# Cross attention L2 written anew: 32-row feature and norm products, new order on all engines

## What is computed

```python
q = _split_heads(queries @ Wq.T); k = _split_heads(keys @ Wk.T); v = _split_heads(values @ Wv.T)
q2 = jnp.sum(q * q, axis=-1); k2 = jnp.sum(k * k, axis=-1)
qk = jnp.einsum('bhsd,bhtd->bhst', q, k)
g_dist = jnp.sqrt(jnp.maximum(q2[..., :, None] + k2[..., None, :] - 2.0 * qk, 0.0)) / DIST_SCALE
compat = (1.0 + g_dist) ** (-(D_INTRINSIC + ALPHA))
N_R = jnp.sum(compat, axis=-1); N_C = jnp.sum(compat, axis=-2)
K_tilde = (N_R ** (-A_EXP))[..., :, None] * compat * (N_C ** (-A_EXP))[..., None, :]
value_weights = K_tilde / jnp.maximum(jnp.sum(K_tilde, axis=-1, keepdims=True), EPS)
attn = jnp.einsum('bhst,bhtd->bhsd', value_weights, v)
...
x = x + _L2_xattn_ref(_layernorm(x, axis=-1), ctx_1024, ctx_1024, ...)
```

## Time and profile before

| | us |
|---|---|
| median of 3 runs | 4875.21 (4873.07 to 4876.48) |
| the profiled execution | 4871.57 |
| its span, first to last instruction | 4869.7 |
| PE busy | 4274.2 (88%) |
| DVE busy | 3812.1 (78%) |
| ACT busy | 3566.7 (73%) |
| POOL busy | 3203.4 (66%) |

### The profile page before, as it was taken

The page is one execution under the profiler, slowest core; times in us unless marked ns, Lnnn a source line. Parts: engine busy times, 40 slices in busy tenths (PEclk is TensorE's granted clock), DMA queues, the critical chain, the costliest instruction groups (busy, mean ns, idle before and its releaser), DMA issues. The chain is left out here.

```text
span 4869.7 us, 153128 instructions
## 1 busy us (share of the span) xinstructions
PE 4274.2 (88%) x50692; PEld 2794.5 (57%) x50694; DVE 3812.1 (78%) x9246; ACT 3566.7 (73%) x13078; POOL 3203.4 (66%) x4063
## 2 busy tenths in 40 slices
PE   6949899988999889998899979998899986677775
PEld 3426566664666646665566646666466664444433
DVE  4779899965999569993899839996599955777488
ACT  6938788974889658884788838887488865777335
POOL 2512399974999569993899929997399952322162
PEclk8969999998999999999899989999999998888986
DMA  2000000000000000000000000000000000000000
GB/s 58 0 19 0 5 2 0 0 19 6 2 0 0 19 7 1 0 0 21 5 0 0 1 24 2 0 0 19 6 2 0 0 19 1 0 0 0 1 27 18
DMA packets 36457, 34.77 MB, mean 7 GB/s; under 512 B 11591, under 2 KB 31301, under 8 KB 35141
## 3 DMA queue, kind: packets, MB, share of 16 engines
q1 hardware_dynamic: 36164, 31.14, 2.2%
HBM read 29.03 MB, written 2.10 MB: 6 GB/s over the span
## 5 line engine op out<-in xcount | busy, mean ns | idle before, releaser
L2479 ACT ACTIVATE local_prob<-ps,local_shift_by 128x128 f32<-128x128 f32 x3072 | 1081.2, 379 | 10.0 <-DVE local_shift_by L2559 9.9
L2407 POOL TENSOR_TENSOR local_qk<-local_qk,local_rsin 128x512 f32<-128x512 f32 x768 | 969.8, 1274 | 57.7 <-DVE local_rsin L2584 57.7
L2414 POOL TENSOR_TENSOR local_qk<-local_qk,local_inv 128x512 f32<-128x512 f32 x768 | 794.4, 1046 | 125.9 <-ACT local_inv L2498 125.3
L2718 PE MATMUL ps<-local_wqkv,local_xsT 128*128 128x512 f32 x1536 | 831.2, 627 | 50.5 <-DVE local_rsin L2584 24.9
L2421 POOL TENSOR_TENSOR local_prob<-local_prob,local_rs 128x512 f32<-128x512 f32 x768 | 792.4, 1044 | 12.6 <-DVE local_rs L2566 12.6
L2479 ACT ACTIVATION_READ_ACCUMULATOR local_prob<-ps,local_shift_by 128x1 f32 x3072 | 673.3, 219 | 0.0
L2573 DVE TENSOR_TENSOR local_qk<-ps,local_cos_t 128x512 f32<-128x512 f32 x768 | 525.3, 684 | 95.3 <-ACT local_sq L2487 92.9
L2559 DVE TENSOR_REDUCE local_shift_by<-ps 128x4 f32<-128x512 f32 x768 | 524.6, 683 | 83.6 <-PE ps L2794 83.6
L2584 DVE TENSOR_TENSOR local_rsin<-ps,local_sin_t 128x256 f32<-128x256 f32 x1536 | 572.1, 414 | 0.0
L2487 ACT ACTIVATE local_sq<-ps 128x512 f32<-128x512 f32 x768 | 467.2, 608 | 101.2 <-PE ps L2718 78.3
L2591 DVE TENSOR_REDUCE local_ss<-local_sq 128x8 f32<-128x512 f32 x768 | 513.1, 669 | 4.9 <-ACT local_sq L2487 4.9
(11 more groups left out here) (332 smaller groups left out, 8849.1 us busy)
## 6 DMA issues: line engine op xcount, KB each, us to landing
local_wqkv<-L_ffn_Wqkv SPq DMA_DIRECT2D x7, 1536.0 KB, 6.7
local_wo<-L_ffn_Wo SPq DMA_DIRECT2D x7, 512.0 KB, 7.3
out<-quantised_res SPq DMA_DIRECT2D x8, 256.0 KB, 2.3
local_w<-L_ffn_W SPq DMA_DIRECT2D x6, 341.0 KB
L_cross_decay<-c_decay SPq DMA_DIRECT2D x1, 1024.0 KB, 12.0
local_w<-L_ffn_W SPq DMA_DIRECT2D x12, 64.0 KB
load_raw<-L_ffn_w SPq DMA_DIRECT2D x8, 64.0 KB, 2.1
local_b<-L_ffn_b SPq DMA_DIRECT2D x24, 0.5 KB
```

Source lines behind the costliest of these rows:

```text
L2407: nc.gpsimd.tensor_tensor(qk[w][:, j, :, :], qk[w][:, j, :, :], rsin[j % 2][:, :, :], ALU.add).then_inc(rot_ready, 1)
L2414: nc.gpsimd.tensor_tensor(qk[w][:, j, :, :], qk[w][:, j, :, :], bcast(inv[:, w, 8 * j:8 * j + 8].unsqueeze(2), [P, 8, LH]), ALU.mult).then ...
L2479: last = nc.scalar.activation(prob[w][:, g, j, :], ps[:, 4 + g % 2, j * P:(j + 1) * P], ACT.Exp, bias=shift_by[:, w, h:h + 1], accum_out=s ...
L2718: nc.tensor.matmul(proj_bank(j), xsT[w][:, :], wqkv[:, 512 * j:512 * j + 512], start=True, stop=True).then_inc(proj_ready, 1)
```

## The change

`cross_attention` is removed and `cross_attention_L2` is written in its place; L0, L1, L3 and all other phases stay as they are, but for their line numbers. In the new phase:

- Features and norms are apart. `fixed` holds k and -2q in full height, `aux` holds the norms and ones, eight rows a head of which two are used. PE's `scores` makes, for a pair of head groups, two 32-row products of features and then two 32-row products of norms into the same banks. POOL makes `spread` and `spread_aux`, 128 by 512 each, with the mask `head_rows`, and also the squares (`squared`).
- The evacuations out of PSUM are shared anew: `xnT`, k, -2q, v and the norms are all taken by DVE, the norms in one operation of 256 columns; ACT reads PSUM only for the logarithm of the row sums. The blocks `vbd` and `nbd` are written by POOL.
- The row sums have a place of their own (`ROWS`, in bank 5 beside `OUT`) and are made two steps ahead of the values. The end of the normalisation is a reciprocal of the weighted sum, `limit`, which takes the smaller of it and 1e12 times the row root, and one product with the values; `num`, `den` and its clamp are gone.
- `work` has two sets, the stages of a tile are spread over more steps, and each engine's order in a step is new. The constant `tile_rows` is gone, `aux_one` replaces two constants, and the selection matrices are new.

```diff
+            def squares(b, w, live):
+                if live(b):
+                    pool.wait_ge(fixed_ready, b + 1)
+                    pool.wait_ge(src_ready, b + 1)
+                    wait(pool, norms_ready, b - 1)
+                    nc.gpsimd.tensor_tensor(squared[:, w, :, :], fixed[:, w, :, :], fixed[:, w, :, :], ALU.mult).then_inc(squares_ready, 1)
...
+            def block_values(b, w, live):
+                if live(b):
+                    pool.wait_ge(rsum_ready, b + 1)
+                    pool.wait_ge(vraw_ready, b + 1)
+                    wait(pool, pv_ready, b - 1)
...
+            def step(n, u, live):
+                v = 1 - u
+                spread_heads(n - 1, v, live)
+                spread_norms(n - 1, v, live)
+                block_values(n - 3, v, live)
+                fetch_context(n, u, live)
+                squares(n, u, live)
+                add_output_bias(n - 4, u, live)
+            sequence_loop(pool, NB, 0, 4, step)
...
+            def step(n, u, live):
+                v = 1 - u
+                columns(n - 4, u, live)
+                second_log(n - 3, v, 0, live)
+                root(n - 3, v, 1, live)
+                powers(n - 3, v, 0, live)
+                log_variance(n, u, live)
+                second_log(n - 3, v, 1, live)
+                first_log(n - 2, u, 0, live)
+                powers(n - 3, v, 1, live)
+                log_rows(n - 4, u, live)
+                log_variance2(n - 6, u, live)
+                over_deviation(n, u, live)
+                root(n - 2, u, 0, live)
+                rows(n - 4, u, live)
+                first_log(n - 2, u, 1, live)
+                log_columns(n - 3, v, live)
+                over_deviation2(n - 6, u, live)
+            sequence_loop(act, NB, 0, 6, step)
...
+            def evacuate_norms(b, w, live):
+                if live(b):
+                    dve.wait_ge(norms_ready, b + 1)
+                    wait(dve, scores_ready, 4 * (b - 1))
+                    nc.vector.tensor_tensor(aux[:, w, :, :], NORMS.rearrange("p (t q) -> p t q", t=2),
+                                            bcast(env["aux_one"][:, :].unsqueeze(2), [P, 2, P]), ALU.add).then_inc(aux_ready, 1)
...
+            def limit(b, w, live):
+                if live(b):
+                    dve.wait_ge(nrow_ready, b + 1)
+                    dve.wait_ge(recip_ready, b + 1)
+                    wait(dve, oT_ready, b - 1)
+                    nc.vector.scalar_tensor_tensor(cut[:, w, :], nrow[:, w, :], 1e12, recip[:, w, :],
+                                                   ALU.mult, ALU.min).then_inc(cut_ready, 1)
...
+            def residual(b, w, live):
+                if live(b):
+                    dve.wait_ge(out_ready, b + 1)
+                    dve.wait_ge(xb_ready, b + 1)
+                    nc.vector.tensor_tensor(tile_of(X, b), xb[:, w, :], OUT, ALU.add).then_inc(x_ready, 1)
...
+            def step(n, u, live):
+                v = 1 - u
+                statistics(n + 6, u, live)
+                evacuate_values(n + 4, u, live)
+                aggregate(n + 6, u, live)
+                evacuate_x(n + 5, v, live)
+                floor(n + 4, u, 0, live)
+                floor(n + 4, u, 1, live)
+                floor(n + 4, u, 2, live)
+                evacuate_spread(n + 5, v, live)
+                evacuate_fixed(n + 5, v, live)
+                column_sums(n + 3, v, 0, live)
+                floor(n + 4, u, 3, live)
+                evacuate_norms(n + 5, v, live)
+                column_sums(n + 3, v, 1, live)
+                norm(n + 6, u, live)
+                one_over_rows(n + 2, u, live)
+                residual(n + 1, v, live)
+                limit(n + 2, u, live)
+                statistics2(n + 1, v, live)
+                evacuate_heads(n + 2, u, live)
+                aggregate2(n + 1, v, live)
+                end_norm(n, u, live)
+            sequence_loop(dve, NB, 6, 0, step)
...
+            def scores(b, w, half, live):
+                if live(b):
+                    pe.wait_ge(spread_ready, b + 1)
+                    pe.wait_ge(spread_aux_ready, b + 1)
+                    pair = (2 * half, 2 * half + 1)
+                    for g in pair:
+                        wait(pe, work_ready, 4 * (b - 1) + g + 1)
+                    for g in pair:
+                        r = slice(32 * g, 32 * g + 32)
+                        nc.tensor.matmul(scores_of(g), fixed[r, w, 0, :], spread[w][r, :, :], start=True, stop=False)
+                    for g in pair:
+                        r = slice(32 * g, 32 * g + 32)
+                        nc.tensor.matmul(scores_of(g), aux[r, w, 0, :], spread_aux[w][r, :, :], start=False,
+                                         stop=True).then_inc(scores_ready, 1)
+
+            def row_sums(b, w, live):
+                if live(b):
+                    pe.wait_ge(prob_ready, 2 * b + 2)
+                    wait(pe, lnrow_ready, b)
+                    wait(pe, x_ready, b - 1)
...
+            def output(b, w, live):
+                if live(b):
+                    pe.wait_ge(oT_ready, b + 1)
+                    wait(pe, x_ready, b)
+                    wait(pe, lnrow_ready, upto(b + 2, NB))
+                    nc.tensor.matmul(OUT, oT[:, w, :], wo[:, :], start=True, stop=True).then_inc(out_ready, 1)
+
+            def step(n, u, live):
+                v = 1 - u
+                weighted_values(n + 1, v, live)
+                norms(n + 4, u, live)
+                output(n, u, live)
+                turn_x(n + 5, v, live)
+                row_sums(n + 2, u, live)
+                scores(n + 4, u, 0, live)
+                scores(n + 4, u, 1, live)
+                project(n + 5, v, live)
+            sequence_loop(pe, NB, 5, 0, step)
```

More of the change, by code:

```diff
@@ L3120, in residual_layers @@
                "X": sb("X", [P, NB * P]), "XN": sb("XN", [P, NB * P]), "Y": sb("Y", [P, NB * P])}
-        for name, shape in (("ident", [P, P]), ("shift", [P, P]), ("head_rows", [P, HG]), ("tile_rows", [P, 2, 8]),
-                            ("aux_sel_fixed", [P, P]), ("aux_sel_spread", [P, P]), ("aux_one_fixed", [P, 1]),
-                            ("aux_one_spread", [P, 1]), ("ones_bd", [P, HG, 32]), ("rotary1", [P, 4, LH]),
+        for name, shape in (("ident", [P, P]), ("shift", [P, P]), ("head_rows", [P, HG]),
+                            ("aux_sel_fixed", [P, P]), ("aux_sel_spread", [P, P]), ("aux_one", [P, 2]),
+                            ("ones_bd", [P, HG, 32]), ("rotary1", [P, 4, LH]),
                             ("band_f", [P, P]), ("band2_f", [P, LH + 96])):
@@ L3178, in residual_layers @@
                   lambda: cross_attention_L1(nc, env, a), layers1,
-                  lambda: cross_attention(nc, env, a, "L2"), lambda: gated_ffn(nc, env, a, 0, "L2"),
+                  lambda: cross_attention_L2(nc, env, a), lambda: gated_ffn(nc, env, a, 0, "L2"),
                   lambda: cross_attention_L3(nc, env, a)]
@@ L3202, in shape_constants @@
     c["c_head_rows"] = ((i[:, None] // DH) % HG == np.arange(HG)[None, :]).astype(f)
-    feature = (i[:, None] // DH) % 8 == np.arange(8)[None, :]
-    norm = i[:, None] % 32 == np.arange(8)[None, :]
-    low_rows = (i < 64)[:, None]
-    c["c_tile_rows"] = np.stack([np.where(low_rows, feature, norm), np.where(low_rows, norm, feature)], 1).astype(f)
-    head_of_row = np.where(i % 32 < 8, i % 32 + 8 * (1 - i // 64), -1)
-    mine = head_of_row[None, :] == (i // DH)[:, None]
-    low = (i % 64 < 32)[None, :]
-    c["c_aux_sel_fixed"] = (mine & low).astype(f)
-    c["c_aux_sel_spread"] = (mine & ~low).astype(f)
-    c["c_aux_one_fixed"] = ((i % 64 >= 32) & (i % 32 < 8)).astype(f)[:, None]
-    c["c_aux_one_spread"] = ((i % 64 < 32) & (i % 32 < 8)).astype(f)[:, None]
+    mine = (i // DH)[:, None] == (i // DH)[None, :]
+    c["c_aux_sel_fixed"] = (mine & (i % DH == 0)[None, :]).astype(f)
+    c["c_aux_sel_spread"] = (0.25 * (mine & (i % DH == 1)[None, :])).astype(f)
+    c["c_aux_one"] = np.stack([i % DH == 1, i % DH == 0], 1).astype(f)
     ones = np.zeros((P, HG, 32), f)
```

932 lines of the change are left out of this document (290 added, 642 removed).

## The result

The changed kernel takes 4785.87 us (median of 4 runs, 4781.67 to 4787.8), the kernel before 4874.18 (4873.07 to 4876.48) beside it: a ratio of 0.9815, 95% interval 0.9803 to 0.9826. The forecast was 4786.0 in a range of 4712 to 4845. The profiled execution took 4787.02 us with a span of 4785.2.

What follows compares the result with a forecast made beforehand. The prediction took a PE and DVE loop through `residual` and `row_sums` as the bound: terms summing to 11.4 us plus 0.57 for the clock, 12.0 a tile; 63 + 28 x T gave 399 us, median 4786, range 4712 to 4845.

Steps and rivals of the forecast that it cites:

- What bounds the kernel now: Old phase: a loop of waits through POOL's spread, the context copy behind it and PE's projections, about 14.4 us a tile.
- The new loop: PE and DVE take turns once a tile: `row_sums` waits for `residual`, which stands behind `evacuate_norms`; 11.4 us.
- Its terms: Pieces of the PE and DVE loop: 1.89 + 0.61 + 0.07 + 2.95 + 0.95 + 4.02 + 0.94 = 11.4 us a tile.
- The slack of 0.25 us on the parallel branch: From the end of `project`, DVE needs 2.25 us to reach `evacuate_norms`, PE 2.5 to give the norms; 0.25 left.
- The clock: PE's 2.8 us gap before `row_sums`: one tile in three pays 1.7 us at half clock, 0.57 on average.
- Start and end: Pipeline two steps deeper: start-up 43 us, tail 20, so phase = 63 + 28 x T.
- The rule that I set against the row: Skill's 3.07 times speedup for four row tiles: scores 2.2 us and T 9.6, where the row gave 4.02.
- Changing the tiling mode: Skill's rule that mode changes drain TensorE: three more changes, some 0.2 us each, 0.6 us a tile, 17 in all.
- VectorE beside POOL: Skill's rule that a 2-port VectorE operation waits for a whole GpSimd instruction: `norm` could wait for `spread_norms`, sum same within tenths.
- Engines: Work a tile in the new phase: DVE some 9.0 us, ACT 9.1 to 9.9, POOL under 6.
- ACT's waits for `work`: Sign to look for in the new phase: ACT waits for `work` 1 us or less a tile.
- Engines' work is the bound: Rival: the engines' work bounds the new phase at about 9.5 us a tile, 329 us, time 4716; chance 0.15.

Runs made afterwards that it cites:

- ctx_first: Kernel before, with POOL's copy of the next tile's context moved ahead of the wide spread: 4874.18 us, period 14.48.
- recip_before: Changed kernel plus one extra unused reciprocal a tile on DVE, between `one_over_rows` and `residual`: 4825.03 us, period 13.11.
- recip_behind: Changed kernel plus the same extra unused reciprocal a tile on DVE, but behind `residual`, ahead of `limit`: 4784.18 us, period 11.80.
- residual_first: Changed kernel with DVE's second column sum and reciprocal moved behind `residual`: 4693.26 us, 0.9628 of the kernel before, period 8.81.
- output_x8: Changed kernel with `output` issuing its product eight times instead of once, filling PE's gap before `row_sums`: 4730.1 us, period 9.97.
- nrow_and_ctx: Kernel before, with POOL's context copy ahead of the spread and ACT's small row steps ahead of the copy of the values: 4872.02 us, period 14.55.
- clamp_folded: Kernel before, with POOL's context copy ahead of the spread and DVE's clamp folded into the product ahead of it: 4846.94 us, period 13.66.
- values_on_dve: Changed kernel with `block_values` moved from POOL back to DVE, behind `aggregate2`: 4783.2 us, period 11.68.
- floor_later: Changed kernel with DVE's third floor moved behind `evacuate_spread` and `evacuate_fixed`: 4781.76 us, period 11.90.
- scores_by_group: Changed kernel with `scores` issuing feature and norm product of each head group directly behind each other: 4784.77 us, period 11.80.

## Why the prediction was right, and where it was not

- *What bounds the kernel now.* That the loop passes through the spread was right; its next step was wrong. The projections' wait for the context copy is real and cost nothing; the link was the clamp, whose long form stood in the earlier trace rows and which I had used for another question. Nothing of the sum for the new kernel rested on it, since the change removes the clamp too, but the expectation of ctx_first did, and failed.
- *The new loop* is as predicted, and recip_before, recip_behind and residual_first show it. The wait of `row_sums` for `residual` is released as said. The gap on PE ahead of it holds the one short transpose.
- *Its terms*, measured at full clock in output_x8 (9.93 us) against the 11.4 of the sum: `project` 0.87 (0.94), values 1.94 (1.89), from the start of `norms` to `row_sums` 3.69 (0.61 + 0.07 + 2.95 = 3.63), `row_sums` 1.01 (0.95). Two terms failed. The scores take 1.94 us, not 4.02: near the lower bound of 1.7 that four side by side would give. The slack of 0.25 us on the parallel branch was not there: its 2.25 us held one floor of four, as if the other three ran beside the scores. They start when these are over, 1.8 us that I had not counted between `project` and `evacuate_norms`. The reason is the first miss itself: four groups side by side finish their four banks at once; with them DVE's branch is as long as PE's and its wait for the squares, 0.42 to 0.49 us. Together the differences are -1.5 us a tile: -2.1 for the scores, +0.5 for that wait, +0.1 for the rest.
- *The clock.* One tile in three was to pay 1.7 us, 0.57 on average. Every tile pays, 1.42 or 2.61 us, 2.0 on average: +1.45. The two misses cancel, and 11.95 us stand beside a forecast of 12.0. Start and end took 401.7 - 28 x 11.95 = 67 us (63 forecast), and the profiled execution 4787 us (4782 forecast); the 3.6 us that I added from there to the median did not come, since the median lies 1.2 below the profiled execution this time. So the time was right within 1 us by luck: the scores were wrong by 2.1 us a tile and the clock by 1.45, in opposite directions, and the smaller misses cancelled too. What the forecast had right is the loop.
- *The rule that I set against the row.* The measured scores at full clock decide for the rule: by my estimate of 6.9 us for one after another, 6.9 / 1.94 = 3.6 times faster. The Trainium skill, "TensorE: Matmul & The Clock Gate", Measured speedup vs the span model, has 3.07, from which I had worked out 2.2 us for the scores; the row that I preferred held a wait. The period of 9.6 that I derived from it would need a clock that holds; output_x8, where it does, has 9.97.
- *Changing the tiling mode.* In output_x8 `row_sums` is modelled to end at 4212.70 and the first 32-row product starts at 4212.63; no drain beyond the ends of the groups is to be seen, and the 0.6 us a tile that I had set against the rule did not come.
- *VectorE beside POOL.* The clamp that meets a running spread instruction ends 0.08 us behind it, in before and in nrow_and_ctx. The Trainium skill, "SBUF — State Buffer", Who interferes with whom, says that a VectorE operation in a 2-port mode, or one with two SBUF inputs, and a GpSimd one that reads SBUF shut each other out for a whole instruction; the traces agree as to the whole instruction, though no run shows in which mode the clamp worked, and clamp_folded shows what it is worth. The `norm` that I had feared for takes 0.34 us in after (4255.84), 0.33 in before.
- *Engines.* DVE 8.7 and ACT 8.9 us a tile (9.0 and 9.1 to 9.9 forecast). ACT's waits for `work` are 2.5 to 3.6 us a tile, not 1: it follows from the floors that start late. They cost nothing as long as the loop is the bound.
- *The rivals.* "Engines' work is the bound" was the only other one that came to exist, in residual_first. It needed the wait for `residual` to go, as the argument against it said.

How the 87.2 us divide among the parts of the change stays open. The clamp and the context copy together are worth 0.9 us a tile (clamp_folded), `block_values` alone none (values_on_dve); what folding the clamp brings without the copy's move was not run; the 32-row products, the joint norms and the deeper pipeline were not taken apart.

## What to carry to other kernels

In a loop between two engines, look at the order within each list: an instruction on which another engine waits should stand ahead of those on which nobody does. Two calls moved behind a third brought 93 us, on top of the 88 of the whole rewriting. Here a gap on PE cost twice, its own length and the slower products behind it, and filling it with useless products paid. Before a row is used as a price, look for waits inside it: merged rows hide them, and an instruction whose duration differs from tile to tile (0.23, 0.82, 1.93 us) may be held by another engine, though it shows as busy.

## What the runs showed of the hardware

- Products of 32 rows in different quarters of the array run side by side whatever their order: sixteen records of 512 columns took 1.94 us at 2.4 GHz (output_x8) and 3.74 at 1.2 GHz (recip_before), against 6.9 and 13.8 one after another by the prediction's estimate. Issuing both products of one quarter directly behind each other changed this by 0.01 us (1.95 and 1.94, 3.60 and 3.60 in tiles of scores_by_group and after).
- PE's clock fell in every tile within the gap of 2.8 us, in turns 2.4 us (4233.1) and 1.2 us (4243.3) after `output` had ended, and returned 3.0 or 5.3 us after `row_sums` had started, in a loop whose instructions are the same each time. Single periods in which it did not fall took 9.92 to 9.95 us in recip_behind, floor_later and scores_by_group, the same as output_x8.
- A clamp from SBUF to SBUF on DVE that meets a running spread on POOL ends 0.08 us behind it (0.73 to 1.93 us instead of 0.23). A product of two SBUF operands is held too (`oT` in nrow_and_ctx: 0.88 us at 4291.20, to 0.15 us behind the end of a spread; 0.29 in before at 4305.12, beside none). The products out of PSUM (281 ns) and the reciprocal (953 ns) beside the same spreads are not held, nor is after's column sum (1.21 us at 4254.72, beside a spread from 4254.88 to 4255.92).
- Eight small block writes are 0.92 us of rows on DVE, 0.76 to the next start, and 1.56 us of rows on POOL.
